# The histogram's row of comparison numbers: SBUF in two bytes, or a PSUM bank in float32

## The reference, cut to what matters

```python
h = batch_norm(x @ w1.T + b1, g1, bt1)
src, dst = (edge_index[0], edge_index[1])
diff = h[src] - h[dst]
m = jax.ops.segment_max(diff, dst, num_segments=N)
m = jnp.where(jnp.isfinite(m), m, 0.0)
hg = jnp.concatenate([h, m], axis=-1)
hg = jax.nn.gelu(batch_norm(hg @ wg.T + bg, gg, btg))
out = batch_norm(hg @ w2.T + b2, g2, bt2) + res
```

## Time and profile before

| | us |
|---|---|
| median of 3 runs | 3400.16 |
| lowest and highest of them | 3392.9 and 3402.04 |
| the profiled execution | 3392.99 |
| its span, first to last instruction | 3391.2 |

### The profile page before, as it was taken

One profiled execution on the slowest core, in us unless ns is written; L12 is line 12 of the kernel. 1 busy time (PEld: TensorE's weight loads), 2 busy tenths in 40 slices (PEclk: granted clock), 3 DMA queues, 4 the chain that ended last, 5 costly groups with the idle time before them and its releaser, 6 DMA issues. The chain is left out here.

```text
span 3391.2 us, 26481 instructions
## 1 busy us (share of the span) xinstructions
PE 1356.8 (40%) x8629; PEld 1200.6 (35%) x8629; DVE 1876.5 (55%) x3453; ACT 713.5 (21%) x770; POOL 1741.9 (51%) x1660
## 2 busy tenths in 40 slices
PE   5200000000000211111121111027889999999998
PEld 5200000000000111111121111026779989998998
DVE  7655655555555555555555555437755555555544
ACT  3100000000000000000000000001546555555554
POOL 3577777777777777777777777753100000000000
PEclk9655555555555555555555555559989999999999
DMA  7856666666566555565566565641032232332321
GB/s 228 292 189 217 229 217 205 207 210 216 192 200 206 196 200 197 197 206 199 193 205 201 198 200 189 204 144 44 17 128 107 102 120 103 120 115 94 123 104 67
DMA packets 173214, 574.95 MB, mean 170 GB/s; under 512 B 32800, under 2 KB 76790, under 8 KB 165908
## 3 DMA queue, kind: packets, MB, share of 16 engines
q1 hardware_dynamic: 95076, 359.62, 28.9%
q0 software_dynamic: 78000, 213.65, 21.2%
HBM read 329.52 MB, written 243.62 MB: 169 GB/s over the span
## 5 line engine op out<-in xcount | busy, mean ns | idle before, releaser
L618 POOL DMA_INDIRECT ring<-ztab,src_i x1566 | 1643.4, 1049 | 498.9 <-issue 475.0
L705 DVE SCALAR_TENSOR_TENSOR ring<-ring,pen 128x256 f32<-128x256 f32 x1566 | 763.8, 488 | 956.7 <-DMA ring<-ztab,src_i 853.1
L823 PE MATMUL ps<-oh_hi,oh_lo 128*128 128x49 bf16 x1566 | 108.1, 217 | 1739.2 <-DVE oh_hi L718 1739.1
L823 PEld LDWEIGHTS ps<-oh_hi,oh_lo 128*128 128x128 bf16 x1566 | 75.6, 116 | 1777.6 <-DVE oh_hi L718 1776.0
L1281 ACT ACTIVATE av<-ps,vecs 128x896 f32<-128x896 f32 x224 | 246.3, 1100 | 348.7 <-PE ps L182 348.6
L716 DVE TENSOR_TENSOR oh_lo<-lo,io_lo 128x768 bf16<-128x768 bf16 (+1 forms) x243 | 247.3, 1018 | 23.1 <-issue 0.9
L1393 DVE TENSOR_TENSOR h2l<-av,h2h 128x896 fp32r<-128x896 f32 x112 | 122.3, 1092 | 213.3 <-ACT h2h L1283 213.3
L1400 DVE SCALAR_TENSOR_TENSOR y<-ps,wv,y 128x256 f32<-128x256 f32 x392 | 168.9, 479 | 111.1 <-PE ps L1574 110.5
L1572 PE MATMUL ps<-fw,h2h 128*128 128x256 f32 x784 | 225.2, 287 | 3.3 <-DVE h2l L1393 3.3
L1573 PE MATMUL ps<-fw,h2l 128*128 128x256 f32 x784 | 222.7, 284 | 0.0
L1574 PE MATMUL ps<-fw,h2h 128*128 128x256 f32 x784 | 222.3, 284 | 0.0
(11 more groups left out here) (234 smaller groups left out, 2548.5 us busy)
## 6 DMA issues: line engine op xcount, KB each, us to landing
runs<-ring SPq DMA_DIRECT2D x261, 768.0 KB, 3.8
fw<-wsp SPq DMA_DIRECT2D x56, 1536.0 KB, 6.5
ring<-ztab,src_i POOLq DMA_INDIRECT x1566, 2.9
res_d<-x_all SPq DMA_DIRECT2D x7, 896.0 KB, 7.9
ztab<-tabc SPq DMA_DIRECT2D x7, 896.0 KB, 5.2
y<-res_d SPq DMA_DIRECT2D x7, 896.0 KB, 7.1
xr<-in_Wx SPq DMA_DIRECT2D x1, 6144.0 KB, 24.7
wsp<-xh SPq DMA_DIRECT2D x8, 768.0 KB, 3.6
```

Source lines behind the costliest of these rows:

```text
L618: pool.indirect_dma_start(ring[:, k, :], None, ztab, bass.IndirectOffsetOnAxis(ap=src_i[:, STEPS * i + k:STEPS * i + k + 1], axis=0)).then ...
L705: r = dve.scalar_tensor_tensor(out=ring[:, k, :], in0=ring[:, before, :], scalar=pen[:, bass.ds(STEPS * i + k, 1)], in1=ring[:, k, :], op0 ...
L823: r = pe.matmul(ps[:, 0, 0:NT], oh_lo[:, j, :], oh_hi[:, j, :], start=False, stop=False)
```

## The change

The row of numbers no longer has tensors of its own in SBUF. `io_lo` and `io_hi` become the first 128 and the next 49 columns of PSUM bank 3, in float32. The two copies that fill them, and the two compares that read them, keep their places, shapes and counts. The bias vector that used bank 3 moves to bank 1. No instruction is added, removed or moved on any engine; SBUF tensors that are laid out behind the two removed ones lie 384 bytes lower.

```diff
-                ("iota", P * 4), ("io_lo", P * 2), ("io_hi", NT * 2 + 2), ("tri", P * 4),
+                ("iota", P * 4), ("tri", P * 4),
...
-        io_lo = plan.at("io_lo", [P, P], BF16, p2["io_lo"])
-        io_hi = plan.at("io_hi", [P, NT], BF16, p2["io_hi"])
+        io_lo, io_hi = ps[:, 3, 0:P], ps[:, 3, P:P + NT]
...
                     dve.tensor_tensor(oh_lo[:, 0:n, :], lo16[:, bass.ds(at, n)].unsqueeze(2).to_broadcast([P, n, P]),
-                                      io_lo[:].unsqueeze(1).to_broadcast([P, n, P]), ALU.is_equal)
+                                      io_lo.unsqueeze(1).to_broadcast([P, n, P]), ALU.is_equal)
                     dve.tensor_tensor(oh_hi[:, 0:n, :], hi16[:, bass.ds(at, n)].unsqueeze(2).to_broadcast([P, n, NT]),
-                                      io_hi[:].unsqueeze(1).to_broadcast([P, n, NT]), ALU.is_equal).then_inc(s_oh, 1)
+                                      io_hi.unsqueeze(1).to_broadcast([P, n, NT]), ALU.is_equal).then_inc(s_oh, 1)
...
-                dve.tensor_copy(io_lo[:], iota[:])
-                dve.tensor_copy(io_hi[:], iota[:, 0:NT])
+                dve.tensor_copy(io_lo, iota[:])
+                dve.tensor_copy(io_hi, iota[:, 0:NT])
...
-                dve.tensor_tensor(dv("bgx"), vec("bg"), ps[:, 3, 0:GM], ALU.add).then_inc(s_bgx, 1)
+                dve.tensor_tensor(dv("bgx"), vec("bg"), ps[:, 1, 0:GM], ALU.add).then_inc(s_bgx, 1)
...
-                        r = pe.matmul(ps[:, 3, m:m + 1], wbq[:, k, m * P:(m + 1) * P], dv("c1", k), start=k == 0, stop=k == KC - 1)
+                        r = pe.matmul(ps[:, 1, m:m + 1], wbq[:, k, m * P:(m + 1) * P], dv("c1", k), start=k == 0, stop=k == KC - 1)
```

## The result

| | before | after |
|---|---|---|
| median | 3401.1 us (4 runs) | 3300.28 us (4 runs) |
| lowest and highest | 3392.9 and 3413.33 | 3299.21 and 3301.12 |
| the profiled execution | 3392.99 | 3301.12 |
| its span | 3391.2 | 3299.4 |

The ratio is 0.9701, with a 95% interval of 0.9671 to 0.973: 100.8 us less by the medians, 91.9 us less between the two profiled executions. The forecast was 3310 us in a range of 3281 to 3335.

What follows compares the result with a forecast made beforehand. GpSimd's back-to-back gathers in stage 2 were taken as the bound. 102 us from faster gathers less 15 for lines 740 and 752 gave 87 us saved: 3396.6 - 87 = 3310 us (rounded), range 3281 to 3335.

Steps and rivals of the forecast that it cites:

- The bound: Stage 2: GpSimd issues gathers back to back, so its length is their number times 1.054 + 0.305 us.
- What the change takes away: Stage 2: the second SBUF input of the 486 compares, which holds up gathers; a PSUM input frees them.
- 102 from the gathers of the last rounds: Rounds 0 to 26: at most 1458 x (1054 - 984) ns saved, 984 ns being gathers in the compare-free last two rounds.
- the scans' share: Stage 2: scans cost 31 ns a gather; a third more or less over 1458 gathers is 15 us.
- The lower bound of 70 us from rounds 9 to 12: Rounds with compares but none of the 22 larger instructions: gathers 1032 ns, so 48 ns x 1458 saved at least.
- two points at which a gather can be held: Stage 2: held gathers ended 0.40 or 0.84 us after a compare; rival of half the hold rested on this.
- the base: Time before the change from which the saving is taken: 3396.6 us, the middle of the four times shown.
- the term for the neighbours: Rounds 0 to 26: 22 larger two-SBUF-input instructions, lines 740 and 752, keep 15 us of the 102.
- The compares' own time: Stage 2, VectorE: each compare changes by 0 to -10 ns, covered by the gathers with 2.8 us to spare.
- Half a hold: Rival for stage 2: a PSUM input frees only one of two holds; 43 us saved, 3353 us; chance 7%.
- none gone: Rival for stage 2: the hold comes from something else; gathers stay at 1054 ns, time 3397 us; chance 7%.
- The third: Rival for stage 2: slower compares make VectorE the bound from 3.2 times their length; 3701 us at four times; chance 4%.

## Why the prediction was right

**The bound.** Right. GpSimd's gathers, back to back, set stage 2: 93.2 us less of them (1643.4 to 1550.2) made 91.9 us less of time.

**What the change takes away.** Right, and shown in four ways: the place and not the type (3391 us with float32 in SBUF), either input (3298 us exchanged), nothing left (3298 us without compares), and the price by itself (0.34 us for another pair in SBUF, none in PSUM).

**The size.** The forecast of 87 us was 102 from the gathers of the last rounds less 15 for lines 740 and 752. The 984 ns of those rounds was close: 991 ns after. Over the 1458 gathers 63 ns each is 92 us, so 10 of the 102 stay and not 15. But the two terms were right in part by luck. By the table above the compares held 104 us, lines 740 and 752 held 6.8 and afterwards 9.8, and the scans' share, which I bounded at a third more or less of 31 ns, rose by 5.1 us, 3.5 ns a gather. The lower bound of 70 us from rounds 9 to 12 would have been a poor choice; the compares fell more kindly there than elsewhere, and those rounds gained only 39 ns a gather, 1032 to 993:

```profile
L617 POOL DMA_INDIRECT ring<-ztab,src_i x205 | 203.6, 993 | 62.5 <-issue 62.5
```

**The way a gather is held.** Wrong in one step, without a price in the sum: I read two points at which a gather can be held, 0.40 and 0.84 us behind the compare. Both were measured from the small compare's end. The first gather was held by the large one alone, and there is one point, 0.83 us behind whatever holds it.

**The level.** The medians differ by 100.8 us and the profiled pair by 91.9. The kernel before scatters over 20 us (3392.9 to 3413.33), the kernel after over 2; I had put the base at 3396.6, and the median turned out to be 3401.1. With 91.9 off 3396.6 one gets 3305. So of the 10 us between 3310 and 3300, about 5 are the term for the neighbours, and the rest is the base, whose scatter I can't explain.

**The compares' own time.** 4 and 5 ns less for the two forms of the large one (6 and 9 for the small one), in the 0 to -10 that was given, and covered: even twice the compares cost nothing.

**The rules weighed.** Of the page "SBUF — State Buffer" of the Trainium skill, section "Who interferes with whom", the runs bear out that two SBUF inputs contend with GpSimd and one doesn't. Its inference that `tensor_tensor` leaves descriptor generation alone does not hold here for an indirect DMA: 1048 ns against 988 by the place of one input. The double rate for bf16 from SBUF that the prediction weighed did not show in these compares before (1092 ns for 896 elements), and none was lost (1087 after).

**The rivals.** Half a hold (3353 us) and none gone (3397 us) are excluded by the time itself, and the two points of hold on which the first of them rested are one point. The third, VectorE as the bound, was placed at 3.2 times the compares' length and 3701 us for four times; the compares made four times over measured 3628. The mechanism is real, and its price was too high by 73 us, of which 68 are that a group takes 9.12 us and not 9.4: the compares take 1.44 us a pair and not 1.5, and the group had been rounded up.

## What to carry to other kernels

Where GpSimd's indirect DMAs are the bound, look in the timeline for VectorE instructions with two inputs in SBUF beside the stretched ones; here a small constant operand in a free PSUM bank cost VectorE nothing and let GpSimd go. Price it from a stretch of the same trace where those instructions don't run, here the last two rounds, rather than from a stretch where they happen to fall well. Measure how far each stretched instruction ends behind every candidate: the true holder shows the same distance each time. Then do the same for the next such instruction: a value carried from step to step can stay in PSUM, if an idle engine copies it out.

## What the hardware showed that I had not expected

- A gather that starts while a VectorE instruction with two SBUF inputs is in flight ends 0.83 us behind it, whether that is a compare, a scan or a larger one; one that started 0.07 us ahead of it takes 0.96 us. The compares still write SBUF after the change and hold nothing, so it is the two inputs that count. A long instruction holds more than in proportion: the large compare had two thirds of the pair's time and 95.9 of its 104 us.
- The kernel before varies by 20 us in its 4 runs and 16 us in the 13 of the next group, the changed one by 2 us in 4. That it is the compares' inputs is not shown: with twice the compares in SBUF 4 runs lie within 6 us.
- In one group of runs TensorE's report to VectorE came late for stretches at a time, and VectorE waited for it up to 59.7 us; the kernel before was about 140 us longer, 127 of it in GpSimd's wait for scans. One-hot tiles without a second buffer make every group wait for that report.
